# One operation over two neighbouring PSUM banks: weighing of the mix, evacuation of y and of the turned tokens

## What is computed

```python
# conv branch
x1 = conv3x3(ln_c(x)[:, :12], w_pc)              # partial convolution, 12 of 48 channels
h  = conv1x1(concat(x1, rest), w_in)             # 48 -> 2 * 127 channels
hf = irfft2(rfft2(patches_8x8(h)) * fft_w)       # spectral weight per channel and frequency
a, b = split(hf)
x  = x + conv1x1(gelu(a) * b, w_out)             # 127 -> 48
# token branch, one token per pixel
t  = ln_t(tokens(x))                             # 48 features
h  = relu(q(t) @ q(W1).T + q(b1))                # 48 -> 192, operands rounded to fp8 e5m2
x  = x + from_tokens(q(h) @ q(W2).T + q(b2))     # 192 -> 48
```

## Time and profile before

| | us |
|---|---|
| median of 3 runs | 757.84 (755.40 to 759.67) |
| the profiled execution's own time | 755.72 |
| span of its trace | 753.9 |
| PE busy | 677.3 (90%) |
| DVE busy | 596.0 (79%) |
| ACT busy | 545.3 (72%) |
| POOL busy | 484.9 (64%) |

### The profile page before, as it was taken

How to read it: one execution, slowest core, us unless ns; L and a number is a source line. 1 busy time by engine, 2 the same in 40 slices (tenths; PEclk the granted TensorE clock), 3 DMA queues, 4 the chain that set the end, 5 groups by cost and what they waited for, 6 DMA issues and landing times.

```text
span 753.9 us, 20168 instructions
## 1 busy us (share of the span) xinstructions
PE 677.3 (90%) x6571; PEld 501.1 (66%) x6571; DVE 596.0 (79%) x1126; ACT 545.3 (72%) x1090; POOL 484.9 (64%) x356
## 2 busy tenths in 40 slices
PE   1249999999999999899999999999999999999952
PEld 1137777767777777667777777677777777776720
DVE  4627788888888888878888888988888888887751
ACT  3133487777877887678788877787878887776764
POOL 2544676767777767767776777777777767743342
PEclk9999999999999999999999999999999999999985
DMA  3332332233332333233333332334433432231001
GB/s 72 76 91 80 79 79 79 78 93 100 103 96 72 101 98 92 68 95 101 102 72 97 96 97 79 78 98 102 102 79 89 103 96 77 71 91 44 22 22 42
DMA packets 46501, 62.36 MB, mean 83 GB/s; under 512 B 19039, under 2 KB 34871, under 8 KB 46391
## 3 DMA queue, kind: packets, MB, share of 16 engines
q1 hardware_dynamic: 46151, 60.94, 31.6%
q10 hardware_dynamic: 240, 0.05, 0.0%
HBM read 44.62 MB, written 16.35 MB: 81 GB/s over the span
## 4 chain that ended last, share of the span: by engine, by line
PE 64%; issue 11%; ACT 8%; DVE 7%; DMA 3%; POOL 3%; SPq 2%; ACTq 1%; POOLq 0%; DVEq 0%
PE mixp L459 15%; PE inva L472 11%; PE invb L477 11%; PE misc L486 7%; PE misc L532 5%; ACT hid L685 4%; PE misc L505 3%; DVE zl L848 3%; PE misc L631 3%; PE misc L514 2%; PE misc L609 2%; ACT zh L729 2%; PE misc L558 2%; PE misc L573 2%; DVE gmix L859 1%
## 5 line engine op out<-in xcount | busy, mean ns | idle before, releaser
L859 DVE TENSOR_TENSOR gmix<-mixp,freq_w 128x508 f32<-128x508 f32 x256 | 163.5, 680 | 36.7 <-PE mixp L459 35.6
L472 PE MATMUL inva<-inv,gmix 128*127 128x128 f32 x1024 | 135.0, 275 | 1.6 <-DVE gmix L859 1.6
L676 ACT ACTIVATE hid<-misc 128x512 f16<-128x512 f32 x192 | 102.0, 621 | 47.1 <-PE misc L532 47.1
L477 PE MATMUL invb<-inv,gmix 128*127 128x128 f32 x1024 | 134.5, 274 | 0.0
L459 PE MATMUL mixp<-win,zh 60*128 60x254 f16 x1024 | 120.0, 272 | 14.3 <-DVE zl L848 12.0
L472 PEld LDWEIGHTS inva<-inv,gmix 128*127 128x127 f32 x1024 | 129.0, 191 | 5.0 <-issue 3.4
L477 PEld LDWEIGHTS invb<-inv,gmix 128*127 128x127 f32 x1024 | 123.8, 191 | 0.0
L1032 POOL TENSOR_TENSOR st<-st,neg_half 128x16 f32<-128x16 f32 x32 | 94.5, 2954 | 45.0 <-DVE st L949 45.0
L459 PE MATMUL mixp<-win,zl 60*128 60x254 f16 x1024 | 118.7, 267 | 0.0
L1063 POOL TENSOR_TENSOR st<-st,neg_half 128x16 f32<-128x16 f32 x32 | 92.8, 2900 | 37.6 <-DVE st L985 37.6
L685 ACT ACTIVATE hid<-hid 128x512 fp8e5<-128x512 f16 x192 | 106.8, 637 | 0.0
(11 more groups left out here) (103 smaller groups left out, 1138.3 us busy)
## 6 DMA issues: line engine op xcount, KB each, us to landing
xin<-in_x_dram SPq DMA_DIRECT2D x64, 192.0 KB, 3.2
xres<-in_x_dram SPq DMA_DIRECT2D x64, 192.0 KB, 3.9
out_dram<-ob SPq DMA_DIRECT2D x64, 192.0 KB, 3.5
taps<-cz_scratch SPq DMA_DIRECT2D x32, 292.5 KB
crm<-rm_scratch SPq DMA_DIRECT2D x64, 96.0 KB
cz_scratch<-cz SPq DMA_DIRECT2D x64, 48.8 KB
cx<-in_x_dram SPq DMA_DIRECT2D x32, 96.0 KB
rm_scratch<-rm_t SPq DMA_DIRECT2D x128, 4.0 KB
```

What stands on the lines that cost most here:

```text
L472: mm = pe.matmul(inva[0:HID, q * PX:(q + 1) * PX], gmix[:, s % 2, q, 0:HID], inv[:], start=True, stop=True, skip_group_check=True)
L477: mm = pe.matmul(invb[0:HID, q * PX:(q + 1) * PX], gmix[:, s % 2, q, HID:HID2], inv[:], start=True, stop=True, skip_group_check=True)
L676: act.activation(hid16[:, 3 * c + g, :], bank[banks[g]][:], ACT.Copy).then_inc(hid16_ready, 1)
L859: dve.tensor_tensor(gmix[:, s % 2, 2 * q:2 * q + 2, 0:HID2], mixp[q][:, 0:2 * HID2].rearrange("p (e c) -> p e c", e=2), freq_w[:], ALU.mul ...
```

## The change

The four PSUM tensors `misc0..3` become one tensor `misc` of four banks, and `mixp0`, `mixp1` one tensor `mixes` of two, so that one access can cross from a bank to its neighbour. Three pairs of operations then become one operation each: the weighing (DVE, 2 x 508 columns to 1016, four times a step), the evacuation of y (ACT, 2 x 512 to 1024) and that of the turned tokens (ACT, 2 x 512 to 1024). Each of them waits for the second of the two increments that its pair waited for one by one, and increments its own semaphore by 2 when all of it is done. Waits of the other engines on these semaphores are as they were. No data is computed otherwise.

```diff
-        bank = [ctx.enter_context(nc.psum_tensor(f"misc{i}", [128, 512], F32)) for i in range(4)]
-        mixp = [ctx.enter_context(nc.psum_tensor(f"mixp{i}", [128, 512], F32)) for i in range(2)]
+        misc = ctx.enter_context(nc.psum_tensor("misc", [128, 4, 512], F32))
+        bank = [misc[:, i, :] for i in range(4)]
+        mixes = ctx.enter_context(nc.psum_tensor("mixes", [128, 2, 512], F32))
+        mixp = [mixes[:, i, :] for i in range(2)]
...
                     act.wait_ge(out_ready, upto(l))
-                    for q in range(2):
-                        act.wait_ge(y_done, upto(2 * l + q + 1))
-                        act.activation(y16[:, 4 * q:4 * q + 4, :].rearrange("p i c -> p (i c)"),
-                                       bank[1 + q][0:SPAN, :], ACT.Copy).then_inc(y16_ready, 1)
+                    act.wait_ge(y_done, upto(2 * l + 2))
+                    act.activation(y16[:].rearrange("p (q i) c -> p q (i c)", q=2), misc[0:SPAN, 1:3, :], ACT.Copy)\
+                       .then_inc(y16_ready, 2)
...
-                    for q in range(2):
-                        act.wait_ge(qT_done, upto(2 * k + q + 1))
-                        act.wait_ge(hid_done, upto(6 * k))
-                        act.activation(q16[:, 4 * q:4 * q + 4, :].rearrange("p i c -> p (i c)"),
-                                       bank[q][0:SPAN, :], ACT.Copy)\
-                           .then_inc(q16_ready, 1)
+                    act.wait_ge(qT_done, upto(2 * k + 2))
+                    act.wait_ge(hid_done, upto(6 * k))
+                    act.activation(q16[:].rearrange("p (q i) c -> p q (i c)", q=2), misc[0:SPAN, 0:2, :], ACT.Copy)\
+                       .then_inc(q16_ready, 2)
...
                 dve.wait_ge(inv_done, upto(8 * n + 2 * s - 2))
-                for q in range(2):
-                    dve.wait_ge(mix_done, upto(8 * n + 2 * s + q + 1))
-                    dve.tensor_tensor(gmix[:, s % 2, 2 * q:2 * q + 2, 0:HID2],
-                                      mixp[q][:, 0:2 * HID2].rearrange("p (e c) -> p e c", e=2),
-                                      freq_w[:], ALU.mult).then_inc(gmix_ready, 1)
+                dve.wait_ge(mix_done, upto(8 * n + 2 * s + 2))
+                dve.tensor_tensor(gmix[:, s % 2, :, 0:HID2].rearrange("p (q e) c -> p q e c", q=2),
+                                  mixes[:, :, 0:2 * HID2].rearrange("p q (e c) -> p q e c", e=2),
+                                  freq_w[:].unsqueeze(1).to_broadcast([128, 2, 2, HID2]), ALU.mult)\
+                   .then_inc(gmix_ready, 2)
```

More of the change, by code:

```diff
@@ L531, in hidden @@
                 r0, r1 = ((0, CH), (HALF, SPAN), (0, SPAN))[g]
-                pe.matmul(dst[:], l1h[r0:r1, g, :], q16[r0:r1, 4 * c:4 * c + 4, :], start=True, stop=True,
+                pe.matmul(dst, l1h[r0:r1, g, :], q16[r0:r1, 4 * c:4 * c + 4, :], start=True, stop=True,
                           skip_group_check=True).then_inc(hid_done, 1)
```

## The result

The changed kernel takes 765.0 us (median of 4 runs, 762.41 to 765.51); the kernel before, with one more run, 756.62 (754.62 to 759.67). The ratio is 1.0083, 95% interval 1.0053 to 1.0113: slower by 6.3 us, between 4.0 and 8.6 (the two medians alone differ by 8.4, and the runs of each kernel spread over 3 and 5 us). That was forecast as to direction (+3.2 us) and lies in the range, but the forecast's sum is half of it. Of the forecast's own cases the likeliest, a change too small to be told from none (under 0.5%, chance 0.57), didn't come; slower (0.37) did.

A forecast was written before the change was run, and what follows sets the result against it. PE, busy 90%, was taken to bound the kernel. Full steps +1.5, fill -0.35 and drain +2.0 sum to +3.2 us, on the median 757.84 giving 761.0 us; range 757.0 to 766.0.

The forecast's parts named there:

- full-step q16: Turned tokens' evacuation on ACT: ends 0.18 us later, but ready about 1 us before L532 in full steps, so +0.
- dearer copies: Upper bound for the merged y16 on ACT: 1.19 us, twice a single copy, making the whole change +7.1 us.
- full steps: Iterations with y and a weigh 0: later y16 delays L935, weigh 0 and residual 0, costing PE +1.5 us.
- POOL's L1024 starts 0.18 later, with 0.5 us of room before POOL's next wait: POOL's addition behind y16: its 0.18 us delay was taken as hidden, at no cost.
- weigh 0's 0.07: Gain of one merged weighing on DVE, 0.07 us, set against y16's 0.18: weigh 0 ends 0.11 later where L935 starts it.
- the 12 steps in which mix 0 sets weigh 0: 12 of 29 iterations: L935's 0.10 us of room leaves +0.01, within the room before L532, so nothing lost.
- The start isn't later: Merged weighing on DVE: it starts no later than the pair, since the two banks' last matmuls run together.
- The drain: Last iterations, nothing covers the two evacuations: 0.5 + 1.09 + 0.38 in iterations 35, 36, 37, together +2.0 us.
- The fill's -0.35: Weighings PE waits for in the first 80 us and two near 712 and 717 us: 5 x -0.07 = -0.35 us.
- Nothing in the full steps: Rival: room before mix 1 and L532 re-forms, only fill and drain remain: +1.65, 759.5 us; chance 0.20.
- The wide copy is no cheaper than two: Rival: merged ACT copy or weighing saves nothing, weigh 0 ends 0.18 to 0.32 later each step: +5 to +11 us; chance 0.17.
- DVE holds the step: Rival: time saved on DVE comes back whole, -7.8 us in full steps, about 752 us in all; chance 0.06.

The follow-up runs named there:

- y16 waiting for both banks: Kernel before, the two y16 copies kept, but the first also waits for the second bank's y_done: ratio 1.0065, +4.9 us.
- L942 early: Changed kernel with only L942 (minus the mean squared) moved ahead of L935 in DVE's order: ratio 1.0057 against the kernel before, +4.3 us.
- y only: Kernel before with only the evacuation of y made one operation: ratio 1.0089, +6.7 us.
- turned tokens only: Kernel before with only the evacuation of the turned tokens made one operation: ratio 1.0004 (0.9984 to 1.0023).
- L883 early: Changed kernel with residual 0 (L883) ahead of the statistics L940 to L949 in DVE's order: ratio 1.0040 against the kernel before.
- L935 late: Changed kernel with DVE's order weigh 0, residual 0, L935, statistics: ratio 1.0429 against the kernel before, +33 us.

## Why the prediction was right, and by half

**Direction and range** held, and so did the mechanism that was named: the merged y16 starts later (0.24 us; taken: 0.21), ends 0.18 later, and this reaches PE through L935 and residual 0. The durations and the untouched full-step q16 came out as worked out. That the total lies in the range is partly luck: the range's upper part was there for dearer copies, and not for a hold by POOL, of which the forecast knew nothing.

**The term that was too small: full steps, +1.5 forecast, 4.3 measured.** The step that failed is the sentence "POOL's L1024 starts 0.18 later, with 0.5 us of room before POOL's next wait". It asked who waits for POOL by semaphore and found nobody. L942 waits for it without one. With that, two things of the forecast's sum fall. First, weigh 0's 0.07 were credited against the 0.18 up to L532; on the way through L1024 there is no such credit. Second, the 12 steps in which mix 0 sets weigh 0 were counted at nothing; L532 hangs on L1024 in them as well, with only their room of 0.05 to 0.13. The mean step from iteration 6 to 35 grew from 20.99 to 21.14 us. In the two sums mix 1 and L532 account for 1.5 + 2.2 = 3.7 of the 4.3 us, `zl` for 0.3 more.

**"The start isn't later" was wrong** for the weighing. The two increments are close, as the x2 row says (0.03 us apart), but behind a mix a wide weighing starts 0.10 later than the pair's first half. Why, beyond those 0.03, is open.

**The drain: +2.0 forecast, 2.1 measured.** Iterations 36 and 37 of the changed kernel:

```profile
740.70 1.03 PE L594 MATMUL misc<-hid,l 128*128 128x512 fp8e5 x2
741.86 1.02 ACT L738 ACTIVATE y<-misc 112x1024 f16<-112x1024 f32 x1 [2.41 <-PE misc L594]
743.13 1.01 PE L611 MATMUL misc<-eye,qpix 128*128 128x128 fp8e5 x8 [1.40 <-ACT y L738]
744.24 1.02 ACT L749 ACTIVATE q<-misc 112x1024 f16<-112x1024 f32 x1 [1.35 <-PE misc L611]
745.40 1.15 PE L534 MATMUL misc<-q,l1h 48*128 48x512 f16 x3 [1.26 <-ACT q L749]
...
755.45 1.02 ACT L738 ACTIVATE y<-misc 112x1024 f16<-112x1024 f32 x1 [2.40 <-PE misc L594]
```

L609 is released by y16 where it was by qpix. From L592's start to L532's it is 4.70 us, before 3.49: 1.21 more (forecast 1.09). Iteration 35 gives 0.50 (0.5), the last y16 0.38 (0.38).

**The fill's -0.35** isn't visible beside the clock's scatter.

**The rivals.** "Nothing in the full steps" fell with the first trace. "The wide copy is no cheaper than two" fell too, though the time came out near its figure for another reason. "DVE holds the step" is half true in a way that wasn't meant: DVE's order and POOL's L1024 hold L532, and DVE's saved time is not on that way.

## What to carry to other kernels

Merging two halves into one operation saves little where the pair overlaps (0.07 and 0.06 us here), and gives up the start on the first half (0.24 us at y in the full steps, 0.45 in the drain); that it pays where the second half is ready as soon as the first isn't shown either: the weighing's halves come 0.03 us apart, and the wide weighing alone gained nothing. Before calling a later POOL operation free, look at what DVE does while it runs: a small operation with two SBUF inputs inside that stretch waits for its end, and shows as a long duration, not as idle time. Put what the bounding engine needs ahead of such an operation, and start the POOL operation early rather than late.

## What the runs showed of the hardware

- A 16-column operation with two SBUF inputs that takes 0.17 us alone took up to 0.43 us when it began 0.2 to 0.4 us before the end of POOL's addition, and 1.54 us when it began 0.62 us into it; where it was held, it ended 0.03 or 0.04 us behind it. A reduction with one SBUF input ran through it unchanged (0.94 us).
- One access over two PSUM banks costs as much as one long access: 1016 columns 1214 ns on DVE (508: 680), 1024 columns 1024 ns on ACT (512: 594).
- The fill isn't the same from run to run: between 55 and 64 us part of the matmuls ran slowly (one mix took 1.87 us instead of 1.05) in 11 of the 14 traces (not in those of the kernel before, of y16 waiting for both banks and of L942 early), and y's first L592 came 1.6 to 4.0 us later in them. In the changed kernel and five more the granted clock shows it (0.5 for 3.4 or 6.8 us near 57). The others, y only and turned tokens only among them, read 1.00 there, though their mixes take the same 1.87 us as in the half-clock stretch.
- Five traces (y only, turned tokens only, y16 waiting for both banks, the changed kernel with L883 early and with L935 late) have another 3.4 us at half clock near 325 or 335 us; the step that holds it is some 1.5 us longer than in the others.
